# First sequence of the attention block: second half of the scores first, six banks, copies by two engines, and an order of its own up to the first ranking

## The chip, the cores and the metric

The kernel runs on one core of one Trainium2 chip. A time is the device time of one execution in microseconds (us). Before the change three runs gave a median of 3631.16 us (3630.14 to 3631.86).

## The reference

A batch of 32 sequences of 256 tokens with 128 channels passes through two blocks, all in float32. Block 0 is a state-space mixer and a feed-forward network, each followed by a layer norm. Block 1, which the change concerns, is attention and another feed-forward network:

```python
q, k, v = heads of x @ Wq, x @ Wk, x @ Wv        # 16 heads of 64
k, v = concat(mem_k, k), concat(mem_v, v)        # 4 memory columns: 260 keys
dots = einsum('bhid,bhjd->bhij', l2norm(q), l2norm(k)) * 10
dots = einsum('hg,bgij->bhij', W_pre_th, dots)   # heads are mixed
dots = where(causal, mask_value, dots)
vk = top_k(dots, 64)[..., -1:]                   # the 64th largest of a row
dots = where(dots < vk, mask_value, dots)
attn = einsum('hg,bgij->bhij', W_post_th, softmax(dots))
out = (attn @ v) * head_scale_params             # then a sigmoid gate, @ Wo
x = layernorm(x + out)
```

## The kernel before

Five engines run five programs that meet only at semaphores. `mixer_phase` (L608) does block 0 for all sequences. `attention_phase` (L1109) then does block 1, one sequence after another in a software pipeline.

Within `attention_phase` a sequence goes through these steps. PE makes the **scores** of 16 heads (`score`, L1407): queries 0 to 127 (half 0, called `blk` 0) against 132 keys in 6 pieces of two or three heads, queries 128 to 255 (half 1) against 260 keys in 16 pieces of one head, into the three banks `FRONT`. ACT copies a piece out of its bank into the buffer `SN`, scaled by the reciprocal norm of the queries (`s_keep`, L1618). SP sends `SN` to a scratch tensor in DRAM, `scores_by_token` (`stage`, L1329), in three pieces for half 0 and four for half 1, and brings it back with heads on the partitions, eight queries by sixteen heads (`regroup`, L1346 and L1348), into the buffer `T8[b % 2]`. A group is 8 queries, there are 32, and two groups form a pair of up to 512 columns. PE **premixes** a pair with W_pre (`premix`, L1422) into one bank, `MIX`; ACT copies it back into `T8` (`t_keep`, L1626); POOL adds the causal mask (`hide`, L1949). The next premix waits until the copy of the last has emptied the bank.

DVE **ranks** the masked scores: eight rankings per sequence (numbered here 0 to 7), each of a quad of four groups, two wide and two narrow. A ranking begins with a `TENSOR_REDUCE` (L1870) and two `TENSOR_TENSOR` (L1803, L1806) and goes on with `MAX8` and `MATCH_REPLACE8` until the 64th value is known. Then ACT takes the row's peak (`peaks`, L1587), POOL drops what is below the threshold (`drop`, L1974 to L1984), ACT takes the exponentials with their sums (`exps`, L1602), DVE the reciprocal of the sums (`share_out`, L1755), POOL scales W_post by it (`share_posts`, L1933), and PE mixes the heads back (L1434, L1438). A ranking waits for work of earlier ones:

```python
if k >= 2:
    dve.wait_ge(dropped, drops(k - 2, 3))
    dve.wait_ge(peaked, k - 1)
```

Beside this the next sequence is prepared: K projected by PE (`k_piece`, L448), squared and summed by ACT (L496), clipped by POOL (`k_clip`, L538), the reciprocal root by ACT and POOL, K scaled by ACT (`k_scale`, L511, tile `ktok`), turned by PE (`k_turn`, L457), all of it in two halves; then Q, whose norms PE sums in `q_turn` (L488), DVE clips in `q_clip` (L566, tile `q_sq`) and ACT and POOL turn into `rq`. The copies of the next scores need `rq`.

What orders this is a table. Each engine runs over periods `p` of 128 beats `t`, and at each beat asks of each step whether it is due (`whose(p, t, beat, lag)`, L1303). A beat is no time: it only says which instruction of an engine stands behind which. In period 1 DVE ranks sequence 0 while PE, ACT, POOL and SP prepare sequence 1; DVE's ranking is cut into 8 slots of 16 beats, and slot n holds ranking n.

For sequence 0 nothing runs beside it that fills the time: DVE waits until its scores have been made, sent, brought back, mixed and masked. `tails` (L1389 on PE, L1578 and L1579 on ACT) makes the last rows of V for all sequences; it stands ahead of the first premix and the first `t_keep`. At the start of the phase POOL clears `T8[0]`, `T8[1]`, `V2` and the three `AT` (L1920 to L1924). `peaks(0, 0)` stands behind ten `t_keep`s of sequence 0, and the remaining six are spread over the period.

Of the kernel before, what the change touches and what calls it, by code (L numbers as in the profile page):

```python
# [12 lines left out]
P = 128  # L13
# [25 lines left out]
S_ALL = len(S_PIECES[0]) + len(S_PIECES[1])  # L39
EXP_LN, SILU, GELU = "natural_log_exp_and_others", "silu_and_others", "gelu_and_others"  # L40
# [378 lines left out]
class Front:  # L419
# [3 lines left out]
    def __init__(self, sh, room, sems, banks):  # L423
# [14 lines left out]
        self.s_kept, self.first_squared = sems.sem("s_kept"), sems.sem("first_squared")  # L438

    def k_piece(self, pe, b, t, f):  # L440
        x = self.xb[b % NXB]
        if t == 0 and f == 0:
            pe.wait_ge(self.x_loaded[b % NXB], 16 * (b // NXB + 1))
            if b:
                pe.wait_ge(self.s_kept, S_ALL * b)
        if t:
            pe.wait_ge(self.k_scaled, 4 * b + f + 1)
# [661 lines left out]
def attention_phase(nc, sh, ctx, out):  # L1109
# [38 lines left out]
    PAIR_AT = {g: (blk * HALF + k) // 2 for blk in range(2) for k, g in enumerate(PREMIX[blk])}  # L1148
# [25 lines left out]

    x_loaded, y_out = front.x_loaded, sems.sems("y_out", 2)
# [4 lines left out]
    zeroed = sems.sem("zeroed")  # L1180
    q_kept, q_clipped, q_root = front.q_kept, front.q_clipped, front.q_root
    s_made, s_kept = sems.sem("s_made"), front.s_kept
# [56 lines left out]
    PE_MIX = (56, 68, 84, 111, 118, 120, 124, 138)  # L1239
    PE_OUT = 35  # L1240
# [71 lines left out]
    def sync(sp):  # L1312
# [8 lines left out]
        def stage(b, blk):  # L1321
# [5 lines left out]
            for n, (lo, hi, pieces) in enumerate(STAGES[blk]):  # L1327
                sp.wait_ge(s_kept, S_ALL * b + S_BEFORE[blk] + pieces)
                sp.dma_start(by_token[blk][:, lo:hi, 0:w], SN[:, lo:hi, 0:w]).then_inc(staged[blk][n], 16)  # L1329

        def regroup(b, blk):

            if b == 1 and blk == 0:
                sp.wait_ge(zeroed, 2)
# [4 lines left out]
            for k in range(HALF // 2):  # L1339
# [10 lines left out]
        for p in range(PERIODS):  # L1350
# [17 lines left out]
            if seq(r):  # L1368
                sp.wait_ge(v_kept, len(WV) * r + 2)
                if r == 0:  # L1370
                    sp.wait_ge(tail_in, 32)
                    sp.wait_ge(zeroed, 2)
# [5 lines left out]
    def tensor(pe):  # L1378
# [14 lines left out]
        def score(b, blk, piece):  # L1393

            n = S_BEFORE[blk] + piece
# [5 lines left out]
            if n >= 2:  # L1401
                pe.wait_ge(s_kept, S_ALL * b + n - 1)
            w = W_LO if blk == 0 else W_HI
            for j, even in enumerate(S_PIECES[blk][piece]):
                for half in range(2):
                    rows = slice(half * DH, (half + 1) * DH)
                    last = pe.matmul(FRONT[(n + half) % 3][:, j * w:(j + 1) * w], qT[rows, even // 2, blk * P:(blk + 1) * P],  # L1407
# [4 lines left out]
        def premix(b, blk, k):  # L1412

            pair = pair_scores(b, PREMIX[blk][2 * k])
            n = 2 * PAIRS * b + PAIRS * blk + k
            if n == 0:
                tails()
# [83 lines left out]

        for p in range(-1, PERIODS):
            for t in range(BEATS):
                for n in range(4):
                    if b := whose(p, t, PE_K[n], 0):
# [35 lines left out]
                for n in range(3):  # L1541
                    if (b := whose(p, t, PE_SCORE0[n], 0)) is not None:
                        score(b, 0, 2 * n)
# [3 lines left out]
                for n in range(8):  # L1547
                    if (b := whose(p, t, PE_SCORE1[n], 0)) is not None:
# [8 lines left out]
                for blk in range(2):  # L1557
                    for k in range(PAIRS):
                        if (b := whose(p, t, PE_PREMIX[blk][k], 0)) is not None:
                            premix(b, blk, k)  # L1560

    def scalar(act):
# [26 lines left out]
        def exps(b, i, pair):  # L1589
# [8 lines left out]
            else:  # L1598
                act.wait_ge(masked, HALF * b + PAIR_AT[QUAD[i][2 * pair]] + 1)
# [4 lines left out]
        def s_keep(b, blk, piece):  # L1604
# [7 lines left out]
            if b and n == 0:  # L1612
# [7 lines left out]

        def t_keep(b, blk, k):
            pair = pair_scores(b, PREMIX[blk][2 * k])
            if (b, blk, k) == (0, 0, 0):
                tails()
            act.wait_ge(premixed, 2 * PAIRS * b + PAIRS * blk + k + 1)
# [44 lines left out]

        for p in range(-1, PERIODS):
            for t in range(BEATS):
                for n in range(4):
                    if (b := whose(p, t, ACT_CTX[n], 2)) is not None:
                        ctx_keep(b, n)
                for n in range(4):
                    if b := whose(p, t, ACT_K[n], 0):
# [16 lines left out]
                for i in range(QUADS):  # L1694
                    if (b := whose(p, t, ACT_PEAK[i])) is not None:
# [21 lines left out]
                for n in range(3):  # L1717
                    if (b := whose(p, t, ACT_SCORE0[n], 0)) is not None:
# [9 lines left out]
                for n in range(8):  # L1728
                    if (b := whose(p, t, ACT_SCORE1[n], 0)) is not None:
# [375 lines left out]
```

## Time and profile before

| what | us |
|---|---|
| median of three runs | 3631.16 |
| the profiled execution, its own time | 3634.36 |
| its span, first to last instruction | 3633.1 |
| DVE busy, share of the span | 3437.1, 95% |
| PE busy | 3390.1, 93% |
| ACT busy | 3092.9, 85% |
| POOL busy | 1745.4, 48% |
| block 1 begins (first instruction of its ACT) | 810.96 |
| first wide step of ranking 0 of sequence 0 | 846.70 |
| mean granted clock of TensorE, share of full speed | 0.98 |

All stretches below are in us from the start of the span. A row of the timeline gives the start, the length of the group, engine, line, operation, output and input with their sizes, how many instructions, and in square brackets how long the engine had been idle before and what released it. A row of busy times gives a stretch, its length, the busy time (and number) of PE, of PE's weight loads, of DVE, ACT and POOL, the granted clock of TensorE as a share of 2.4 GHz, the busy share of the DMA engines and the GB/s they moved.

### The profile page before, as it was taken

Reading aid. Unit: us, or ns where it says so; the run is one execution under the profiler, and the core shown is the slowest. Engines: PE = TensorE matmul, PEld = TensorE weight load, DVE = VectorE, ACT = ScalarE, POOL = GpSimd, SP = SyncE. Lnnn points to the kernel's source line nnn. Section 1 sums busy time; section 2 is a strip of 40 time slices with the busy share of each in tenths; the row PEclk is TensorE's granted clock in tenths of the full one; section 3 lists DMA queues with packets and bytes.
Section 4 is the critical chain, followed back from the end, with each engine's and each line's share of the span. In section 5 each row is a group of like instructions: output and inputs, shape, how many; then the busy total and the mean of one; then the engine's idle time right before and its main releaser. Section 6 shows DMA issues by size and latency. Waiting matters only on the chain.

```text
span 3633.1 us, 78764 instructions
## 1 busy us (share of the span) xinstructions
PE 3390.1 (93%) x19287; PEld 2527.5 (70%) x19287; DVE 3437.1 (95%) x18664; ACT 3092.9 (85%) x10837; POOL 1745.4 (48%) x3670
## 2 busy tenths in 40 slices
PE   4999999986999999999999999999999999999987
PEld 2888888863666666676676666666666666666665
DVE  7999999936999999999999999999999999999993
ACT  6888888856898899989899898998998998898863
POOL 0000000014666666666666666666666666666663
PEclk9999999997999999999999999999999999999998
DMA  3000000002222222222222222222222222222210
GB/s 132 11 14 13 13 12 13 10 13 85 73 71 78 82 66 65 65 66 66 66 65 66 74 71 70 74 73 79 79 66 65 65 66 65 67 65 66 73 55 4
DMA packets 254141, 210.74 MB, mean 58 GB/s; under 512 B 78000, under 2 KB 234736, under 8 KB 252912
## 3 DMA queue, kind: packets, MB, share of 16 engines
q1 hardware_dynamic: 253680, 205.70, 18.1%
q8 instruction: 154, 2.52, 0.3%
q14 instruction: 307, 2.51, 0.2%
HBM read 93.97 MB, written 111.67 MB: 57 GB/s over the span
## 4 chain that ended last, share of the span: by engine, by line
PE 66%; ACT 17%; DVE 11%; issue 4%; POOL 2%; DMA 0%; SPq 0%; DVEq 0%; ACTq 0%; POOLq 0%
PE bank L378 10%; PE bank L221 8%; PE bank L1434 6%; PE bank L1422 5%; PE bank L1407 5%; PE bank L1465 3%; PE bank L469 3%; PE bank L195 3%; ACT SN L1618 3%; PE bank L1499 3%; DVE W L1826 3%; PE bank L1479 3%; PE bank L1438 3%; PE bank L346 3%; ACT sq L496 2%
## 5 line engine op out<-in xcount | busy, mean ns | idle before, releaser
L1826 DVE MATCH_REPLACE8 W<-last,W 128x130 f32<-128x130 f32 (+18 forms) x3456 | 871.9, 259 | 0.0
L1848 DVE MAX8 last<-W 128x8 f32<-128x130 f32 (+18 forms) x3456 | 762.9, 262 | 0.0
L1933 POOL TENSOR_SCALAR posts<-post,share 128x128 f32<-128x128 f32 x1024 | 366.7, 378 | 284.0 <-DVE share L1755 279.1
L1602 ACT ACTIVATE T<-T,peak 128x260 f32<-128x260 f32 (+15 forms) x1024 | 410.9, 409 | 3.5 <-POOL T L1984 2.4
L1618 ACT ACTIVATE SN<-bank,rq 128x260 f32<-128x260 f32 (+1 forms) x1024 | 357.9, 424 | 61.3 <-PE bank L1407 60.8
L1422 PE MATMUL bank<-T,pre 128*128 128x40 f32 (+15 forms) x1024 | 365.3, 439 | 14.4 <-ACT T L1626 10.1
L1434 PE MATMUL bank<-posts,T 128*128 128x128 f32 (+7 forms) x2048 | 311.7, 289 | 68.9 <-POOL posts L1933 60.6
L1984 POOL TENSOR_TENSOR T<-T,below 128x520 f32<-128x520 f32 (+12 forms) x416 | 360.3, 882 | 20.0 <-DVE below L1857 4.6
L1434 PEld LDWEIGHTS bank<-posts,T 128*128 128x128 f32 (+7 forms) x2048 | 249.0, 174 | 165.3 <-POOL posts L1933 88.9
L938 DVE TENSOR_TENSOR_SCAN hs<-dA,dx 128x256 f32<-128x256 f32 x512 | 349.9, 684 | 2.9 <-ACT dA L800 1.9
L1949 POOL TENSOR_TENSOR T<-T,w_mask 128x32 f32<-128x32 f32 x512 | 141.1, 278 | 412.6 <-ACT T L1626 410.2
L1407 PE MATMUL bank<-kT,qT 64*128 64x260 f32 (+1 forms) x2048 | 275.7, 373 | 43.3 <-ACT SN L1618 33.9
L538 POOL TENSOR_SCALAR k_sq<-k_sq 128x16 f32<-128x16 f32 x64 | 17.7, 276 | 564.7 <-DVE k_sq L551 514.3
L1974 POOL TENSOR_SCALAR below<-T,last 128x244 f32<-128x244 f32 (+3 forms) x256 | 269.6, 1053 | 33.6 <-DVE last L1846 10.3
L1422 PEld LDWEIGHTS bank<-T,pre 128*128 128x128 f32 x1024 | 168.7, 192 | 164.6 <-issue 84.6
L1826 DVE MATCH_VALUE_LOAD W<-last,W 128x8 f32 x3456 | 262.6, 76 | 0.0
L221 PE MATMUL bank<-f_b,w_f1h 128*128 128x256 f32 x1024 | 248.6, 386 | 5.7 <-ACT f_b L233 5.7
L1626 ACT ACTIVATE T<-bank 128x40 f32<-128x40 f32 (+15 forms) x512 | 208.2, 407 | 49.6 <-PE bank L1422 47.1
L1571 ACT ACT_TABLE_LOAD x192 | 246.3, 1283 | 4.6 <-POOLq L1100 1.1
L221 PE MATMUL bank<-f_a,w_f1h 128*128 128x256 f32 x1024 | 247.7, 385 | 0.0
L800 ACT ACTIVATE dA<-delta,neg_a 128x256 f32<-128x256 f32 x512 | 237.5, 502 | 8.8 <-DVE delta L1067 8.4
L1407 PEld LDWEIGHTS bank<-kT,qT 64*128 64x128 f32 x2048 | 146.9, 191 | 136.5 <-ACT SN L1618 76.2
(242 smaller groups left out, 9572.3 us busy)
## 6 DMA issues: line engine op xcount, KB each, us to landing
scores_by_token<-SN SPq DMA_DIRECT2D x64, 520.0 KB, 2.6
scores_by_token<-SN SPq DMA_DIRECT2D x64, 396.0 KB, 3.1
scores_by_token<-SN SPq DMA_DIRECT2D x32, 780.0 KB, 3.3
scores_by_token<-SN SPq DMA_DIRECT2D x32, 264.0 KB, 2.6
scores_by_token<-SN SPq DMA_DIRECT2D x32, 260.0 KB, 2.0
T<-scores_by_token SPq DMA_DIRECT2D x32, 244.0 KB, 3.0
T<-scores_by_token SPq DMA_DIRECT2D x32, 228.0 KB, 3.2
T<-scores_by_token SPq DMA_DIRECT2D x32, 212.0 KB, 3.8
```

What stands on the lines that cost most here:

```text
L221: last = pe.matmul(o[:, (m % 2) * SEQ:(m % 2 + 1) * SEQ], self.w[layer][:, c, m * P:(m + 1) * P], src[:, c, :], start=c == 0, stop=c == HC ...
L378: last = pe.matmul(o[:, (m % 2) * SEQ:(m % 2 + 1) * SEQ], self.w[layer][:, c, m * P:(m + 1) * P], src[:, c, :], start=c == 0, stop=c == HC ...
L938: dve.tensor_tensor_scan(hs[j % NH][:], dA[j % ND][:], dx[b % 2][:], 0.0, ALU.mult, ALU.add).then_inc(scanned, 1)
L1407: last = pe.matmul(FRONT[(n + half) % 3][:, j * w:(j + 1) * w], qT[rows, even // 2, blk * P:(blk + 1) * P], kT[rows, even // 2, 0:w], star ...
L1422: pe.matmul(MIX[:, 0:pair.shape[-1]], pre[:], pair, start=True, stop=True).then_inc(premixed, 1)
L1434: return pe.matmul(at0[0:m, j * P:(j + 1) * P], scores(b, QUAD[i][j], 0, m), posts[(n + j) % NP][:], start=True, stop=True)
L1602: act.activation(one, one, ACT.Exp, bias=peak[k % 2][:, j:j + 1], accum_out=total[k % 4][:, j:j + 1]).then_inc(e_made, 1)
L1618: last = act.activation(SN[:, h, 0:w], FRONT[n % 3][:, j * w:(j + 1) * w], ACT.Copy, scale=rq[:, c:c + 1])
L1826: dve.match_replace(both[:, s, at:to], best[n], both[:, s, at:to], LOWEST).then_inc(ranked, 1)
L1848: dve.max(best[n], both[:, s, at:to]).then_inc(ranked, 1)
L1933: pool.tensor_scalar(posts[(4 * k + j) % NP][:], post[:], share[k % 2][:, j:j + 1], 1.0, ALU.mult, ALU.mult).then_inc(posts_made, 1)
L1984: pool.tensor_tensor(x, x, out, ALU.add).then_inc(dropped, 1)
```

## The change

It concerns sequence 0 of block 1, and the steps of sequence 1 that are prepared beside its ranking.

1. **Scores.** Half 1 is made before half 0. Six banks are used in turn, where it was three. Even pieces are copied by ACT, odd ones by DVE, which did not copy scores. Half 0 goes to a buffer of its own, a part of `T8[1]`, so that its copies do not wait until `SN` has been sent.
2. **SP.** Half 1 is sent first (four pieces), then half 0 (three). The pairs then come back one by one, of half 1 and of half 0 in turn.
3. **Premix.** All 16 premixes, `t_keep`s and `hide`s of sequence 0 stand directly behind the scores on PE, ACT and POOL, pairs of half 1 and half 0 in turn. The first half of sequence 1's K is projected and squared ahead of them. On POOL the first `drop` stands behind the twelfth `hide`.
4. **Clearing.** `T8[1]` and `V2` are cleared by DVE, `T8[1]` once half 0 has been sent.
5. **Order behind it.** `tails` stands behind `peaks(0, 0)` on ACT and behind the last premix on PE. `peaks(0, 1)`, the first `share_out`, the first `drop` of ranking 1 and `q_clip` of sequence 1 have beats of their own.

The core of the diff:

```diff
+FIRST_SCORES = [(blk, piece) for blk in (1, 0) for piece in range(len(S_PIECES[blk]))]
...
+    FIRST = [(blk, k) for k in range(QUADS) for blk in (1, 0)]
+    FIRST_SN = (T8[1][:, 0:HEADS * W_LO].rearrange("p (h n) -> p h n", h=HEADS), SN)
+    FIRST_BANK = [*FRONT, *ATB, BACK[1]]
+    TAILS = 12
+    FIRST_PEAK, FIRST_SHARE, FIRST_CLIP = 24, 62, 68
...
             if seq(f):
-                stage(f, 0)
-                regroup(f, 0)
-                stage(f, 1)
-                regroup(f, 1)
+                if f:
+                    for blk in range(2):
+                        stage(f, blk)
+                        regroup(f, blk)
+                else:
+                    stage(0, 1)
+                    stage(0, 0)
+                    for blk, k in FIRST:
+                        regroup(0, blk, (k,))
...
+        for blk, piece in FIRST_SCORES[::2]:
+            score(0, blk, piece)
+        for f in range(2):
+            front.k_piece(pe, 1, 0, f)
+        for blk, k in FIRST:
+            premix(0, blk, k)
         for p in range(-1, PERIODS):
             for t in range(BEATS):
+                if (p, t) == (1, TAILS):
+                    tails()
...
+        first_keep()
+        for f in range(2):
+            front.k_square(act, 1, 0, f)
+        for blk, k in FIRST:
+            t_keep(0, blk, k)
...
+        dve.wait_ge(q_root.stepped, Root.STEPS)
+        for n, (blk, piece) in enumerate(FIRST_SCORES):
+            if n % 2:
+                dve.wait_ge(s_made, n + 1)
+                w = (W_LO, W_HI)[blk]
+                for j, h in enumerate(S_PIECES[blk][piece]):
+                    c = blk * HEADS + h
+                    last = dve.tensor_scalar(FIRST_SN[blk][:, h, 0:w], FIRST_BANK[n % 6][:, j * w:(j + 1) * w], rq[:, c:c + 1], None, ALU.mult)
+                last.then_inc(s_halved, 1)
+        dve.memset(V2[:], 0.0)
+        for sent in staged[0]:
+            dve.wait_ge(sent, 16)
+        dve.memset(T8[1][:], 0.0).then_inc(blanked, 1)
...
-        pool.memset(T8[1][:], 0.0)
-        pool.memset(V2[:], 0.0)
...
+        for blk, k in FIRST:
+            hide(0, blk, k)
+            if (blk, k) == (0, 5):
+                turn_over(0, 0)
+                drop(0, 0)
```

ACT, from the first `t_keep` of half 1 to the first `k_scale` (`T_0` is `T8[0]`, `peak` is the step `peaks`, `ktok` the scaled K, `k_t` and `rk` its root). Before:

```order
L1626 ACTIVATE T_0<-bank 128x512
L78 ACTIVATE k_t<-k_sq 128x16
L80 ACTIVATE rk<-k_t 128x16
L1626 ACTIVATE T_0<-bank 128x488
L1587 ACTIVATE peak<-top 128x4
L511 ACTIVATE ktok<-bank,rk 128x64 x16
```

After, from the sixth `t_keep` from the end:

```order
L1673 ACTIVATE T_0<-bank 128x360
L1673 ACTIVATE T_0<-bank 128x200
L1673 ACTIVATE T_0<-bank 128x328
L1673 ACTIVATE T_0<-bank 128x232
L1673 ACTIVATE T_0<-bank 128x296
L1673 ACTIVATE T_0<-bank 128x264
L79 ACTIVATE k_t<-k_sq 128x16
L81 ACTIVATE rk<-k_t 128x16
L1624 ACTIVATE peak<-top 128x4
L1615 ACTIVATE V<-bank 128x512
L1616 ACTIVATE V<-bank 128x512
L1624 ACTIVATE peak<-top 128x4
```

Here `L514 ACTIVATE ktok` follows directly. The root of K and the first peak stand behind all sixteen `t_keep`s, where they stood behind nine and ten; the two copies of `tails` stand ahead of `ktok`.

DVE, from the last instruction of block 0 to the first ranking (`SN` and `T_1`, which is `T8[1]`, take the copies). Before:

```order
L566 TENSOR_SCALAR q_sq<-bank 128x32
L1870 TENSOR_REDUCE top<-T_0 128x2
L1803 TENSOR_TENSOR W<-T_0 128x2x130
L1806 TENSOR_TENSOR W<-T_0 128x2x130
L1814 MAX top<-W 128x8 x2
```

After:

```order
L569 TENSOR_SCALAR q_sq<-bank 128x32
L1948 TENSOR_SCALAR SN<-bank,rq 128x260 x8
L1948 TENSOR_SCALAR T_1<-bank,rq 128x132 x8
L1950 MEMSET V 128x1024
L1953 MEMSET T_1 128x4480
L1924 TENSOR_REDUCE top<-T_0 128x2
L1857 TENSOR_TENSOR W<-T_0 128x2x130
```

Sixteen copies and two memsets stand ahead of ranking 0.

DVE in ranking 4, from its `TENSOR_REDUCE` to `q_clip` of sequence 1 (`neg` is a negated narrow group). Before:

```order
L1870 TENSOR_REDUCE top<-T_0 128x2
L1803 TENSOR_TENSOR W<-T_0 128x2x98
L566 TENSOR_SCALAR q_sq<-bank 128x32
L1806 TENSOR_TENSOR W<-T_0 128x2x98
L1814 MAX top<-W 128x8 x2
```

After:

```order
L1924 TENSOR_REDUCE top<-T_0 128x2
L1857 TENSOR_TENSOR W<-T_0 128x2x98
L1860 TENSOR_TENSOR W<-T_0 128x2x98
L1868 MAX top<-W 128x8 x2
L1880 MATCH_REPLACE W<-top,W 128x98 x2
L1824 MAX last<-neg 128x8
L1902 MAX last<-W 128x8 x2
L1832 MATCH_REPLACE W<-last,neg 128x76
L1832 MATCH_REPLACE W<-last,neg 128x84
L1880 MATCH_REPLACE W<-last,W 128x98
L569 TENSOR_SCALAR q_sq<-bank 128x32
```

`q_clip` stands behind eleven more instructions of ranking 4.

## Rows read from the trace of the kernel before

**Rows 1.** Busy time by stretches: the long middle, when DVE ranks sequences 1 to 31.

```profile
930.00:3490.00 2560.00, 2454.93 (x15015) 1761.09 (x15013) 2531.22 (x15994) 2308.68 (x8954) 1622.30 (x3429) 1.00 0.22 69
```

**Rows 2.** Timeline of DVE: rankings 0, 2 and 4, q_clip, first ranking of sequence 1.

```profile
846.70 0.43 DVE L1803 TENSOR_TENSOR W<-T 128x260 f32<-128x260 f32 x1 [21.00 <-POOL T L1949]
...
866.40 0.25 DVE L1870 TENSOR_REDUCE top<-T 128x2 f32<-128x104 f32 x1
...
883.94 0.32 DVE L1870 TENSOR_REDUCE top<-T 128x2 f32<-128x168 f32 x1
...
884.44 0.19 DVE L566 TENSOR_SCALAR q_sq<-bank 128x32 f32<-128x32 f32 x1
...
932.46 0.43 DVE L1803 TENSOR_TENSOR W<-T 128x260 f32<-128x260 f32 x1 [0.36 <-POOL T L1949]
```

**Rows 3.** Timelines of PE, ACT and POOL: scores, their copies, clearing.

```profile
811.07 0.94 PE L1407 MATMUL bank<-kT,qT 64*128 64x132 f32 x12 [1.97 <-POOLq L1100]
...
829.00 1.24 PE L1407 MATMUL bank<-kT,qT 64*128 64x260 f32 x4
...
827.20 0.85 ACT L1618 ACTIVATE SN<-bank,rq 128x260 f32<-128x260 f32 x2 [0.83 <-PE bank L1407]
...
811.21 3.83 POOL L1920 MEMSET T<- 128x4480 f32 x1
```

**Rows 4.** Timeline of SP's queue: sending half 0, bringing halves 0 and 1 back.

```profile
815.45 3.24 SPq L1329 DMA_DIRECT2D scores_by_token<-SN  x3
...
821.85 3.95 SPq L1348 DMA_DIRECT2D T<-scores_by_token  x8
...
841.50 3.50 SPq L1348 DMA_DIRECT2D T<-scores_by_token  x7
```

**Rows 5.** Busy time by stretches: sending half 0, half 1, and three of PE's.

```profile
818.00:819.00 1.00, 1.00 (x4) 0.34 (x5) 0.00 (x0) 0.30 (x2) 1.00 (x2) 0.50 1.13 288
829.00:830.00 1.00, 1.00 (x5) 0.50 (x4) 0.00 (x0) 0.28 (x1) 0.25 (x1) 0.50 1.01 424
826.00:842.00 16.00, 13.40 (x37) 6.71 (x38) 0.00 (x0) 6.89 (x19) 1.73 (x7) 0.50 0.42 155
843.00:850.00 7.00, 3.96 (x8) 0.89 (x6) 3.30 (x20) 6.07 (x40) 2.60 (x10) 1.00 0.93 287
...
863.00:867.00 4.00, 4.00 (x15) 3.13 (x13) 4.00 (x22) 2.62 (x11) 0.34 (x1) 0.54 0.01 2
```

**Rows 6.** Timelines of PE and ACT: tails, a premix at half clock, at full.

```profile
819.00 3.62 PE L1389 MATMUL bank<-w_wv,gate 128*128 128x512 f32 x4
...
837.59 1.03 PE L1422 MATMUL bank<-T,pre 128*128 128x200 f32 x2
...
844.57 1.12 PE L1422 MATMUL bank<-T,pre 128*128 128x512 f32 x2 [0.83 <-DMA T<-scores_by_token]
...
838.66 0.34 ACT L1626 ACTIVATE T<-bank 128x200 f32<-128x200 f32 x1
...
845.74 0.60 ACT L1626 ACTIVATE T<-bank 128x512 f32<-128x512 f32 x1
```

**Rows 7.** Timelines of ACT, POOL and PE: K and Q of sequence 1.

```profile
848.20 3.39 ACT L511 ACTIVATE ktok<-bank,rk 128x64 f32<-128x64 f32 x16
...
860.27 3.39 ACT L511 ACTIVATE ktok<-bank,rk 128x64 f32<-128x64 f32 x16 [0.75 <-POOL rk L90]
...
856.63 1.51 POOL L1984 TENSOR_TENSOR T<-T,below 128x520 f32<-128x520 f32 x1 [4.27 <-DVE below L1857]
...
876.84 0.51 PE L488 MATMUL bank<-w_stack,qn 128*128 128x16 f32 x4
```

**Rows 8.** Timeline of ACT: sequence 1's first copies and first `t_keep` of half 1.

```profile
886.64 1.64 ACT L1618 ACTIVATE SN<-bank,rq 128x132 f32<-128x132 f32 x6
...
907.95 0.85 ACT L1618 ACTIVATE SN<-bank,rq 128x260 f32<-128x260 f32 x2 [4.08 <-PE bank L1407]
...
930.22 0.67 ACT L1626 ACTIVATE T<-bank 128x512 f32<-128x512 f32 x1
```

More of the change, by code:

```diff
@@ L445, in k_piece @@
                 pe.wait_ge(self.s_kept, S_ALL * b)
+                pe.wait_ge(self.s_halved, S_ALL // 2)
         if t:
@@ L1327, in stage, with regroup @@
             for n, (lo, hi, pieces) in enumerate(STAGES[blk]):
[L1328 to L1331 removed]
+                if b:
+                    sp.wait_ge(s_kept, S_ALL * b + S_BEFORE[blk] + pieces)
+                else:
+                    kept = FIRST_SCORES.index((blk, 0)) + pieces
+                    sp.wait_ge(s_kept, kept)
+                    sp.wait_ge(s_halved, kept // 2)
+                by_head = SN if b else FIRST_SN[blk]
+                sp.dma_start(by_token[blk][:, lo:hi, 0:w], by_head[:, lo:hi, 0:w]).then_inc(staged[blk][n], 16)
+        def regroup(b, blk, pairs=range(HALF // 2)):
             if b == 1 and blk == 0:
[L1334 removed]
+                sp.wait_ge(blanked, 1)
             if b >= 2 and blk == 0:
@@ L1338, in regroup @@
                 sp.wait_ge(sent, 16 * (b + 1))
-            for k in range(HALF // 2):
+            for k in pairs:
                 g = PREMIX[blk][2 * k]
@@ L1406, in score @@
                     rows = slice(half * DH, (half + 1) * DH)
-                    last = pe.matmul(FRONT[(n + half) % 3][:, j * w:(j + 1) * w], qT[rows, even // 2, blk * P:(blk + 1) * P],
+                    last = pe.matmul((FRONT[(n + half) % 3] if b else FIRST_BANK[(n + half) % 6])[:, j * w:(j + 1) * w], qT[rows, even // 2, blk * P:(blk + 1) * P],
                                      kT[rows, even // 2, 0:w], start=True, stop=True)
@@ L1541, in tensor @@
                 for n in range(3):
-                    if (b := whose(p, t, PE_SCORE0[n], 0)) is not None:
+                    if b := whose(p, t, PE_SCORE0[n], 0):
                         score(b, 0, 2 * n)
@@ L1547, in tensor @@
                 for n in range(8):
-                    if (b := whose(p, t, PE_SCORE1[n], 0)) is not None:
+                    if b := whose(p, t, PE_SCORE1[n], 0):
                         score(b, 1, 2 * n)
@@ L1676, in scalar @@
                 for n in range(4):
-                    if b := whose(p, t, ACT_K[n], 0):
+                    if (b := whose(p, t, ACT_K[n], 0)) and (b > 1 or n >= 2):
                         front.k_square(act, b, n // 2, n % 2)
@@ L1694, in scalar @@
                 for i in range(QUADS):
-                    if (b := whose(p, t, ACT_PEAK[i])) is not None:
+                    if (b := whose(p, t, FIRST_PEAK if i == 1 and p == 1 else ACT_PEAK[i])) is not None:
                         peaks(b, i)
@@ L1717, in scalar @@
                 for n in range(3):
-                    if (b := whose(p, t, ACT_SCORE0[n], 0)) is not None:
+                    if b := whose(p, t, ACT_SCORE0[n], 0):
                         s_keep(b, 0, 2 * n)
@@ L1728, in scalar @@
                 for n in range(8):
-                    if (b := whose(p, t, ACT_SCORE1[n], 0)) is not None:
+                    if b := whose(p, t, ACT_SCORE1[n], 0):
                         s_keep(b, 1, 2 * n)
@@ L1898, in vector @@
                 for i in range(QUADS):
-                    if (b := whose(p, t, DVE_SHARE[i])) is not None:
+                    if (b := whose(p, t, FIRST_SHARE if i == 0 and p == 1 else DVE_SHARE[i])) is not None:
                         share_out(QUADS * b + i)
@@ L1904, in vector @@
                     nc_.dve_finish(dve, b, x_c[:])
-                if b := whose(p, t, DVE_Q_CLIP, 0):
+                if b := whose(p, t, FIRST_CLIP if p == 1 else DVE_Q_CLIP, 0):
                     front.q_clip(dve, b)
@@ L1999, in gpsimd @@
                 for i in range(QUADS):
-                    if (b := whose(p, t, POOL_TURN[i])) is not None:
+                    if (b := whose(p, t, POOL_TURN[i])) is not None and (b, i) != (0, 0):
                         turn_over(b, i)
-                    if (b := whose(p, t, POOL_DROP[i])) is not None:
+                    if (b := whose(p, t, POOL_DROP[0 if i == 1 and p == 1 else i])) is not None and (b, i) != (0, 0):
                         drop(b, i)
```

61 lines of the change are left out of this document (39 added, 22 removed).

## The prediction

> **What bounds the kernel now.** I read the busy times of the long middle first. Between 930 and 3490 DVE is busy 2531.22 of 2560 us, 98.9%, and PE 95.9% [rows 1]. So from sequence 1's first ranking to the end DVE's rankings set the pace, and the time of the kernel is the start of that ranking plus a stretch that the change does not touch. Call the first wide step of sequence 1's ranking R1: it began at 932.46 [rows 2]. **A microsecond is won only if R1 comes earlier by one.** A measurement of this kernel can tell about 0.2% from no change, which is 7.3 us.
>
> Then the timeline of DVE ahead of R1. Ranking 0 of sequence 0, call its first wide step R0, began at 846.70 after 21.00 us of idleness [rows 2]; from there to R1 DVE hardly waits. That idle time is what the change is after. The timelines of SP, PE and ACT show what it consists of: clearing before the first send, half 0 sent and brought back before half 1 is sent [rows 4], scores and copies that pass three banks, at TensorE's lower clock level [rows 3, 5]. The last thing to read is what else stands between R0 and R1: the chain that prepares K and Q of sequence 1 on the other engines [rows 7, 8]. R1 needs both.
>
> **Part 1: R0 comes about 12.7 us earlier.** The scores begin at 811.07 as before. A score group for two 260-wide pieces takes 1.24 at half clock, its two copies on ACT 0.85 [rows 3]. With six banks and two copying engines PE no longer waits for banks: 8 groups by 1.24 are 9.9 us for half 1, at full clock about half. That two engines copy means that copies follow PE. DVE's copy from a bank is in no row of before; bounds are 0 and ACT's 0.43 apiece, and neither end binds, since 8 of them by 0.43 lie beside 5 to 10 us of PE. By the errata section of the Trainium skill's page "VectorE: DVE Perf Modes" (VectorE, source in PSUM) such a copy would take (120 + 260) cycles at 0.96 GHz, 0.40 us, an estimate that leaves the sum as it is.
>
> The transfers are what is left. The queue's first send waits for POOL's first clearing, 811.21 + 3.83 = 815.04 [rows 3]; the first send was issued at 815.45 [rows 4]. Half 1 is 256 x 16 x 260 x 4 / 2 = 2.13 MB, and the part sent at 829 moved at 424 GB/s; half 0 is 1.08 MB and moved at 288 [rows 5]. From 816.1: 0.45 (another load ahead of it) + 5.0 + 3.75 = 825.3; landing and its signal add about 1, so half 0 is complete near 826.2 (with 288 GB/s for both halves 828.6, with 424 for both 825). Then the first narrow pair is issued with about 0.5 and the first wide pair, which came back 3.07 us after its issue at 841.50 (issue in [rows 4], premix at 844.57 in [rows 6]): first premix 829.8. Two pairs must be mixed before ranking 0. At half clock two matmuls of w columns take 0.36 + 0.0032w (0.0032 from the four 512-wide ones, 3.62 us; 0.36 from the 200-wide pair, 1.03), the copy 0.17 + 0.00083w (0.34 and 0.60), 0.1 for the two handovers [rows 6]. 512 columns: 2.7. 40 columns: 0.8. A mask and its handovers 0.6. **R0 = 833.9, 12.8 earlier.** DVE's clearing of `T8[1]` lies in this stretch (826.2 to at most 831.6; POOL's takes 3.83 [rows 3]) and is hidden by the transfer and the first premix; without that cover it would be 4 to 5 us.
>
> **Part 2: sequence 1's K comes later.** Before, the first peak and the root of K stood behind ten and nine `t_keep`s; now both stand behind all sixteen, and these go through one bank one after another: no premix begins before the copy of the last. Widths sum to 8 x 552 + 56 = 4472. At half clock PE takes 16 x 0.36 + 4472 x 0.0032 = 20.1, ACT 16 x 0.17 + 4472 x 0.00083 = 6.4, handovers 1.6: **28.1 us**, 829.8 to 857.9. At full clock the 512-wide pair takes 1.12 [rows 6]; with 0.30 + 0.0016w PE takes 12.0 and the chain 20.0.
>
> Which clock? In the score stretch, 13.40 us busy of 16, it stayed at 0.50; under an uninterrupted PE (863 to 867) it rose; at 843 to 850 PE was busy 57% and it stayed at 1.00 [rows 5]. The chain comes out of several idle us of PE, so it begins at the lower level, and it keeps PE at 20.1 / 28.1 = 72%, less than in the stretch that stayed low. I take half clock and keep the other as a rival.
>
> Behind the last `t_keep`: root of K and first peak by 858.9; `tails`, 3.62 on PE [rows 6] plus copies, until 861.8; then the first `ktok`, which began at 848.20 [rows 7]: **+13.6**. The second began at 860.27, 12.07 later, of which POOL's first `drop` at 856.63 held the clipping up by about 2.7 [rows 7]; that drop now lies earlier, so the second `ktok` is at 861.8 + 9.4 = 871.2, +10.9. Behind it the chain to `q_turn` (876.84) is PE's and ACT's own work; one premix of 0.8 us has left it: q_turn near 887, and q_clip can run at about 888.
>
> **Part 3: DVE waits in the middle instead.** Unhindered, DVE would reach ranking 2 at 833.9 + 19.7 = 853.6. It needs the first peak, 858.9: a wait of 5.3. Ranking 4 (883.94 - 866.40 = 17.5 later: 876.4) needs the third peak, which stands behind the turned K on ACT, near 881: 4.6. q_clip stands 2.3 us further into ranking 4 than before (eleven instructions) and would be reached at 884; it waits for q_turn until about 888: 4. Together 14 us of new waits against 12.8 won. q_clip to R1 was 932.46 - 884.44 = 48.0 with a wait of 0.36 in it; less 2.3 that now lies ahead, 45.4. **By DVE's own work R1 = 933.5, +1.**
>
> **Part 4: sequence 1's scores.** Their copies need `rq`, behind q_clip and behind the gates, which follow q_turn: they began at 886.64 [rows 8] and now begin near 895.7, +9.1. From there to the first wide `t_keep`, 930.22 [rows 8], lie 43.6 us of copies, sending and mixing. Part of that were waits for PE and POOL whose work follows DVE's rankings (these come only 1 to 3 us later), so the chain can catch up, to some +4 at the `t_keep`: R1 = 932.46 + 4 = 936.5. This is later than 933.5, so it decides. **Sum: 3631.2 + 4 = 3635.2 us**; the profiled execution, 3634.36 by its own time, would be 3638.4. I forecast 3635.
>
> **Rivals.**
> - *Full clock in the mixing chain.* The chain would end 8.1 earlier, at 849.8, first peak 850.8, ahead of ranking 2, K and Q some +3 instead of +11. R1 near 930.3: -2.2, 3629. For it: at 843 to 850 a PE busy for only 57% kept the upper level [rows 5]. Against it: the idle PE ahead of the chain. Beside this stands the Trainium skill, "TensorE: Matmul & The Clock Gate", section "HAM oscillation": matmuls in bursts with waits between them lose the upper clock and run at half of it; the row at 826 to 842 agrees for scores, the one at 843 to 850 does not.
> - *The gain holds.* If the first peak, the third peak and q_turn come before DVE asks for them, R1 moves by all of R0's 12.8: 3618.4; with half of the waits 3624. It needs the K chain to be 10 us faster than its rows; for it speaks only that the chain has gaps of 1 to 5 us in the trace which could close, and that its work is spread over more engines.
> - *Slower.* The copies of sequence 1's scores begin 9.1 late and do not catch up: their place is ACT's queue behind the gates, where each later copy has scores, exponentials and peaks of earlier rankings ahead of it. Then R1 = 932.46 + 9.1 and the time 3640.3. It decides from a catching up of less than 2 us (3638.4 is the bound of slower). For it: PE and ACT are busy 96% and 90% of the long middle [rows 1] and have little to catch up with. Against it: within those 43.6 us ACT waited 4.08 for PE at 907.95 [rows 8], and there PE was waiting in turn for work that follows DVE.
> - *It doesn't do what it says.* If sending the two halves takes turns with other traffic and R0 is only 5 us earlier, the chain of part 2 begins later too, and the time goes the slower way; it is in that case's chance.
>
> **Chances.** Forecast (half clock, R1 +1 to +7) 0.52; full clock, 3629, 0.17; gain holds wholly or by half 0.13; slower 0.18. So faster by over 0.2% 0.13, within 0.2% 0.69, slower by over 0.2% 0.18. The range takes in the first two, the half of the gain's nearer end and the price of the slower rival: 3625 to 3641.
>
> **What would show it.** R0 near 834 in DVE's timeline; sixteen premixes between 830 and 858 at a granted clock of 0.50; the first peak at 859 and DVE idle about 5 us ahead of ranking 2, again ahead of ranking 4, and before q_clip; `ktok` at 862 and 871; sequence 1's first copies near 896; R1 near 936. Wrong would be: an upper clock in the chain, DVE without waits between R0 and R1, or R1 before 928.

## The result and the profile after

Twelve runs of the change had a median of 3640.76 us, twelve of the kernel before beside them 3630.65. The ratio is **1.0024, 95% interval 1.0014 to 1.0034**, so the change costs 5 to 12 us, 8.7 at its middle. A second comparison, on another set of runs, gave 1.0025 (1.0013 to 1.0037). The median lies in the stated range (3625 to 3641) by 0.24 us. Its ratio is on the slower rival's side of the 0.2% bound, not the forecast's, though the interval reaches across that bound.

The single profiled executions hide this: 3634.36 us before, 3634.72 after. What the change does must be read ahead of R1, the first wide step of sequence 1's ranking. I give times from **start**, the first table load of the attention block on ACT (810.96 before, 810.43 after), because it moves from one execution to the next: over all thirteen profiles of this record it lies between 809.05 and 813.25.

| from start, us | before | forecast | after |
|---|---|---|---|
| R0, first wide step of ranking 0 | 35.7 | 22.9 | 23.9 |
| copy of the sixteenth pair ends | – | 46.9 | 49.0 |
| first peak | 37.0 | 47.9 | 50.3 |
| first scaled K | 37.2 | 50.8 | 53.1 |
| second scaled K | 49.3 | 60.2 | 63.5 |
| `q_clip` of sequence 1 | 73.5 | 77 | 78.8 |
| first copies of sequence 1's scores | 75.7 | 84.7 | 86.2 |
| first wide `t_keep` of sequence 1 | 119.3 | 123.3 | 126.8 |
| R1 | 121.5 | 125.5 | 129.0 |

The forecast's clock times stand here less 810.96. R1 is 7.5 us later in place of 4, and that is nearly all of the 8.7. (A second profile of each kernel, below, has 122.3 and 128.6, so R1 itself is known to some 0.8 us; the two means are 6.9 apart.)

The timeline of DVE in the kernel after, the rows with a wait and R0 (they answer to [rows 2]):

```profile
834.22 0.20 DVE L1924 TENSOR_REDUCE top<-T 128x2 f32<-128x40 f32 x1 [2.62 <-POOL T L2014]
834.33 0.42 DVE L1857 TENSOR_TENSOR W<-T 128x260 f32<-128x260 f32 x1
...
861.05 0.26 DVE L1924 TENSOR_REDUCE top<-T 128x2 f32<-128x104 f32 x1 [7.99 <-issue]
...
883.26 0.18 DVE L1809 RECIPROCAL share<-total 128x4 f32<-128x4 f32 x1 [4.62 <-ACT T L1639]
...
886.11 0.33 DVE L1924 TENSOR_REDUCE top<-T 128x2 f32<-128x168 f32 x1 [1.77 <-POOL T L2049]
...
889.24 0.19 DVE L569 TENSOR_SCALAR q_sq<-bank 128x32 f32<-128x32 f32 x1 [0.22 <-PE bank L491]
...
901.13 0.57 DVE L1911 TENSOR_SCALAR below<-T,last 128x196 f32<-128x196 f32 x2 [5.32 <-POOL T L2049]
...
939.46 0.43 DVE L1857 TENSOR_TENSOR W<-T 128x260 f32<-128x260 f32 x1 [0.34 <-POOL T L2014]
```

Read from above: R0 is 11.8 us earlier from start, as wanted. Then DVE waits 7.99 ahead of ranking 2, 4.62 for the first share, 1.77 ahead of ranking 4, 0.22 at `q_clip` and 5.32 inside ranking 4: 19.9 us at places where it had not waited in the kernel before. The profile puts the 7.99 down to no engine; the first peak on ACT ended at 860.96, just ahead of it (next view). 19.9 - 11.8 is 8.1; R1 moved by 7.5.

PE and ACT, timelines, at both ends of the row of sixteen and behind it ([rows 6, 7]):

```profile
817.88 1.96 PE L451 MATMUL bank<-w_wk,xb 128*128 128x512 f32 x4 [1.26 <-DVE T L1948]
830.14 2.07 PE L1451 MATMUL bank<-T,pre 128*128 128x512 f32 x2 [10.31 <-DMA T<-scores_by_token]
833.00 0.62 PE L1451 MATMUL bank<-T,pre 128*128 128x40 f32 x2 [0.78 <-ACT T L1673]
833.91 1.99 PE L1451 MATMUL bank<-T,pre 128*128 128x488 f32 x2 [0.29 <-ACT T L1673]
...
857.80 1.25 PE L1451 MATMUL bank<-T,pre 128*128 128x264 f32 x2 [0.51 <-ACT T L1673]
858.84 3.62 PE L1417 MATMUL bank<-w_wv,gate 128*128 128x512 f32 x4
```

```profile
859.09 0.39 ACT L1673 ACTIVATE T<-bank 128x264 f32<-128x264 f32 x1 [1.34 <-PE bank L1451]
...
860.77 0.19 ACT L1624 ACTIVATE peak<-top 128x4 f32<-128x4 f32 x1
862.50 0.60 ACT L1615 ACTIVATE V<-bank 128x512 f32<-128x512 f32 x1 [1.54 <-PE bank L1417]
...
863.57 3.38 ACT L514 ACTIVATE ktok<-bank,rk 128x64 f32<-128x64 f32 x16
...
873.88 3.38 ACT L514 ACTIVATE ktok<-bank,rk 128x64 f32<-128x64 f32 x16 [0.75 <-POOL rk L91]
```

Each premix waits for the copy of the one before, each copy for its premix. The busy times show the clock in it: PE is busy 18.95 us of 27, at 0.50 throughout:

```profile
832.00:859.00 27.00, 18.95 (x32) 7.99 (x32) 18.74 (x100) 6.06 (x15) 5.12 (x16) 0.50 0.17 45
```

Last, POOL's timeline ahead of the wait that I had not forecast, at 901.13:

```profile
895.22 0.24 POOL L85 TENSOR_TENSOR q_t<-rq 128x32 f32<-128x32 f32 x1 [9.15 <-ACT rq L81]
...
896.53 2.09 POOL L2039 TENSOR_SCALAR below<-T,last 128x212 f32<-128x212 f32 x2
898.67 0.15 POOL L2044 MEMSET below<- 128x68 f32 x1
898.92 0.52 POOL L2041 TENSOR_SCALAR below<-neg,last 128x68 f32<-128x68 f32 x1
899.52 1.51 POOL L2049 TENSOR_TENSOR T<-T,below 128x424 f32<-128x424 f32 x2
```

POOL stood idle for 9.15 us, waiting for the root of sequence 1's query norms, which comes from ACT behind the gates and two table loads. Behind that root in POOL's queue is the drop of ranking 3, whose values had been there since DVE ended that ranking at 884.3, and for that drop DVE waited.

The chain of sequence 1 on ACT, its first score copies and its first wide `t_keep` ([rows 8]):

```profile
896.63 1.64 ACT L1655 ACTIVATE SN<-bank,rq 128x132 f32<-128x132 f32 x6
...
937.24 0.68 ACT L1673 ACTIVATE T<-bank 128x512 f32<-128x512 f32 x1
```

Between them lie 40.6 us, where the kernel before had 43.6.

### The profile page after: what moved, and what is told of

It reads as the page before. It is cut to its first block, busy times and chain, and to the rows that moved or that the text cites. A ratio compares the mean times of both kernels' runs of the same rounds, so it can differ in the third digit from the quotient of the medians.

```text
span 3633.4 us, 78806 instructions
## 1 busy us (share of the span) xinstructions
PE 3381.3 (93%) x19287; PEld 2520.0 (69%) x19287; DVE 3449.5 (95%) x18682; ACT 3085.4 (85%) x10821; POOL 1732.8 (48%) x3668
## 4 chain that ended last, share of the span: by engine, by line
PE 60%; DVE 17%; ACT 16%; issue 5%; POOL 2%; DMA 0%; SPq 0%; DVEq 0%; ACTq 0%; POOLq 0%
PE bank L379 9%; PE bank L222 7%; PE bank L1463 5%; PE bank L1451 5%; DVE W L1880 5%; PE bank L1438 4%; DVE last L1902 3%; PE bank L472 3%; PE bank L1494 3%; PE bank L196 3%; PE bank L1528 3%; ACT sq L499 2%; PE bank L1508 2%; ACT SN L1655 2%; PE bank L1467 2%
## 5 line engine op out<-in xcount | busy, mean ns | idle before, releaser
L1451 PE MATMUL bank<-T,pre 128*128 128x392 f32 (+15 forms) x1024 | 371.0, 445 | 25.1 <-ACT T L1673 12.3
L1655 ACT ACTIVATE SN<-bank,rq 128x132 f32<-128x132 f32 (+1 forms) x992 | 345.6, 423 | 52.6 <-PE bank L1438 52.2
L1438 PE MATMUL bank<-kT,qT 64*128 64x260 f32 (+1 forms) x2048 | 267.7, 366 | 38.6 <-ACT SN L1655 32.3
L1673 ACT ACTIVATE T<-bank 128x512 f32<-128x512 f32 (+15 forms) x512 | 207.6, 405 | 75.8 <-PE bank L1451 73.9
L379 PE MATMUL bank<-f_b,w_f0h 128*128 128x256 f32 x1024 | 241.4, 379 | 0.0
```

What stands on the lines that cost most here:

```text
L379: last = pe.matmul(o[:, (m % 2) * SEQ:(m % 2 + 1) * SEQ], self.w[layer][:, c, m * P:(m + 1) * P], src[:, c, :], start=c == 0, stop=c == HC ...
L1438: last = pe.matmul((FRONT[(n + half) % 3] if b else FIRST_BANK[(n + half) % 6])[:, j * w:(j + 1) * w], qT[rows, even // 2, blk * P:(blk + ...
L1451: pe.matmul(MIX[:, 0:pair.shape[-1]], pre[:], pair, start=True, stop=True).then_inc(premixed, 1)
L1655: last = act.activation(SN[:, h, 0:w], FRONT[n % 3][:, j * w:(j + 1) * w], ACT.Copy, scale=rq[:, c:c + 1])
```

## The experiments

Three questions: what moves R1, which part of the front wins the 11.8 us, and why the clock stayed low. Edits are shortened, and against the change where nothing else is said. Ratios are to the kernel before; R1 and R0 are from start, from each kernel's profile (the change: 129.0 and 23.9).

### DVE's waits one by one

```diff
-if (b := whose(p, t, POOL_DROP[0 if i == 1 and p == 1 else i])) is not None ...:
+if (b := whose(p, t, POOL_DROP[0 if i == 1 and p == 1 else i] - 3 * (i == 3 and p == 1))) is not None ...:
     drop(b, i)
```

> On POOL, the drop of sequence 0's ranking 3 stands ahead of the root of sequence 1's query norms instead of behind it; nothing else differs from the change. In the profile of the change DVE waited 5.3 us for that drop inside ranking 4, at 901.13, and the drop stood in POOL's queue behind the root (895.22). Start means the first table load of the attention block on ACT (810.43 there), R1 the first wide step of sequence 1's first ranking (939.46, start + 129.0); before the change it was start + 121.5. Theory A (the scores of sequence 1 set R1, DVE's waits only fill the time until then): the 5.3 us vanish but the same time is waited at R1, R1 stays at start + 129 to 130, time about 3640. Theory B (DVE's own waits set R1): R1 at start + 123.7, time 5 us shorter, about 3635.

Ratio 1.0033 (1.0021 to 1.0045), R1 at 127.6. The 5.32 us are gone from DVE's timeline, and two others have come, 2.06 ahead of ranking 5 and 2.14 for a share just ahead of R1:

```profile
898.21 0.36 DVE L1924 TENSOR_REDUCE top<-T 128x2 f32<-128x200 f32 x1 [2.06 <-issue]
...
935.62 0.18 DVE L1809 RECIPROCAL share<-total 128x4 f32<-128x4 f32 x1 [2.14 <-ACT T L1639]
...
938.33 0.43 DVE L1857 TENSOR_TENSOR W<-T 128x260 f32<-128x260 f32 x1 [0.64 <-POOL T L2014]
```

Of 5.3 us 1.4 reach R1 (1.0 against the second profile of the change), and the time is no shorter. Removing a wait of DVE's does not move the chain of sequence 1: its first wide `t_keep` is at 126.6 from start, as in the change (126.8), and R1 can't come before it. The 1.4 lie mostly behind that `t_keep`. In the change its mask stood in POOL's queue behind a scaling of W_post that waited for DVE (937.33 to 938.75) and began at 939.18, 128.8 from start; here it begins at 127.3.

```diff
 for blk, k in FIRST:
     t_keep(0, blk, k)
+    if (blk, k) == (0, 1):
+        peaks(0, 0)
+    if (blk, k) == (0, 5):
+        peaks(0, 1)
```

> On ACT, the first two peaks of sequence 0 stand inside the row of sixteen copies (behind the fourth and the twelfth) instead of behind all of them; nothing else differs. The 8.0 us that DVE waited ahead of ranking 2 should vanish under any theory. Theory A (the chain that starts with sequence 1's K, behind the sixteen copies, sets everything until R1): the waits for the first share and ahead of ranking 4 grow by the same 8 us, R1 stays at start + 129, time about 3640. Theory B (waits of DVE add up): 8 us shorter, about 3632.

(Both peaks are taken out of the place where they stood.) Ratio 1.0035 (1.0023 to 1.0047), R1 at 130.1. Ahead of ranking 2 DVE now waits 0.71, but 3.96 in ranking 2 and 8.45 in place of 4.62 for the first share. Theory A again: R1 stays (it is 1.1 later), and the time stays with it. DVE gets no further than the chain of sequence 1 lets it.

### The row of sixteen

```diff
-pe.matmul(MIX[:, 0:pair.shape[-1]], pre[:], pair, ...)
+pe.matmul((MIX if b or n % 2 == 0 else BACK[0])[:, 0:pair.shape[-1]], pre[:], pair, ...)
```

The copy reads the same bank, and a premix waits for the copy of the pair before the last.

> The sixteen premixes of sequence 0 use two banks in turn, so that PE mixes a pair while ACT copies the one before; nothing else differs. In the change they took from 830.14 to 859.5, 29.3 us, with PE busy about 72% at half clock. Theory A (this row of sixteen, one bank, moves sequence 1's K and with it R1): at half clock the row is PE's own 20 to 21 us, the last copy near 851, sequence 1's first scaled K 8.5 us earlier, R1 7 to 8.5 us earlier (start + 121 to 122), time 3632 to 3633. If PE, now without gaps, is granted the full clock during it, the row takes about 15 and the gain is up to 12 us. Theory B (R1 is late for another reason, POOL's queue or the first rankings): R1 within 2 us of start + 129, time 3638 to 3640.

Ratio 0.9995 (0.9986 to 1.0005), **R1 at 114.0**, 15.0 us earlier than in the change by an edit that touches nothing but the row:

```profile
924.73 0.43 DVE L1857 TENSOR_TENSOR W<-T 128x260 f32<-128x260 f32 x1 [0.36 <-POOL T L2014]
```

The row takes 16.3 us in place of 29.3, and the first scaled K is at 38.9 in place of 53.1. With smaller gaps PE also got its upper clock:

```profile
834.00:838.00 4.00, 3.58 (x8) 1.85 (x6) 4.00 (x25) 0.82 (x3) 0.46 (x2) 0.50 0.71 194
838.00:842.00 4.00, 3.23 (x10) 1.70 (x8) 3.96 (x22) 1.57 (x5) 1.21 (x4) 0.78 0.01 2
842.00:846.00 4.00, 3.29 (x12) 2.10 (x13) 3.96 (x20) 1.95 (x7) 2.75 (x7) 1.00 0.02 6
```

So the expectation's case with the upper clock is the one that came, and its "up to 12 us" was too low. How the 15 us divide between overlap and clock was not measured apart; at half clock the expectation had 7 to 8.5.

Undoing that part, only ten pairs in a row and six where they stood before:

```diff
-for blk, k in FIRST:
+for blk, k in FIRST[:10]:
     t_keep(0, blk, k)
...
+    elif b == 0 and blk and k >= 2:
+        t_keep(0, *FIRST[8 + k])
```

(the same on PE and POOL, where the first `drop` stands behind the tenth `hide`)

> Undoes one part of the change: only the first ten of sequence 0's sixteen premixes, copies and masks stand in a row, the last six stand at the beats at which the last six stood before the change (one bank, as in the change). Start is the first table load of the attention block, R1 the first wide step of sequence 1's first ranking: start + 121.5 before the change, + 129.0 in the change. Theory A (sequence 1's K waits behind the row, and everything until R1 follows it): the row ends 11 us earlier, near start + 38, the first scaled K begins near + 42.5 instead of + 53.1, R1 at + 119 to 121, 8 to 10 us less than in the change, time a little below the kernel before (3622 to 3630 where that gives 3626 to 3631). Theory B (the total of the sixteen counts, wherever they stand, because the later six delay K's second half and Q by as much): R1 at + 126 or later, time 5 us or more above the kernel before.

R1 at 121.8, 7.2 earlier than in the change; first scaled K at 44.5. Theory A in kind, but 1 to 3 us less than it had said. The ratio, 1.0016 (1.0008 to 1.0025), missed the expectation by more: R1 stands where it stood in the kernel before, and the runs are 3 to 9 us longer. I come back to this below.

### The clock

```diff
+for _ in range(12):
+    pe.matmul(ATB[0][:], pre[:], sh.wv[:, 0:512], start=True, stop=True)
 for blk, k in FIRST:
     premix(0, blk, k)
```

> Twelve more matmuls of 512 columns into a free bank, whose results nobody reads, stand on PE between the K projection and the first premix, where PE idled for 10.3 us; nothing else differs. They keep PE busy until about 829.5 if the clock is full all along. Theory A with the clock as its cause: the row of sixteen starts at the full clock, and at a share of busy time of about 60% keeps it; it takes 20 to 22 us instead of 29.3, R1 is 6 to 8 us earlier, time about 3633. Rival (the clock falls inside the row, because PE has a gap behind every pair): the granted clock drops to 0.50 within the first few pairs, the row takes 27 us or more, R1 and the time stay within 2 us of the change, 3638 to 3640.

Ratio 1.0026 (1.0015 to 1.0036), R1 at 128.0. The added matmuls ended 1.2 us later, from start, than the change's first premix began. The row, now 27.1 us, did begin at the full clock, and lost it:

```profile
834.00:838.00 4.00, 2.67 (x7) 0.84 (x6) 2.37 (x6) 1.02 (x3) 0.51 (x2) 1.00 0.95 261
838.00:842.00 4.00, 2.54 (x4) 0.99 (x4) 3.96 (x26) 1.15 (x3) 0.51 (x2) 0.56 0.57 152
842.00:846.00 4.00, 2.94 (x6) 1.43 (x6) 4.00 (x21) 0.78 (x2) 0.88 (x3) 0.50 0.00 0
```

The rival was right: this row, with a gap behind each pair, did not keep the clock that it was given. The Trainium skill's page "TensorE: Matmul & The Clock Gate", section "A second HAM failure mode: psum-queue depth-cycling", tells of a kernel in which PE cycles through banks with small idle times between groups of matmuls and goes back and forth between its two clock levels. The trace agrees with the fall; here there is one, from 1.00 at 834 to 838 to 0.50 at 842 to 846, and no rise after it until the row ends. My prediction's rival of a full clock in the mixing chain is thereby excluded twice, in the change itself and with a warm start.

### K out from behind the row

```diff
+front.k_guess(act, 1, 0)
+front.k_scale(act, 1, 0)
+front.k_keep(act, 1, 0, 0)
 for n, (blk, k) in enumerate(FIRST):
     t_keep(0, blk, k)
+    if n == 1:
+        front.k_square(act, 1, 1, 0)
...
+    if n == 8:
+        front.k_scale(act, 1, 1)
```

(and the matching steps on PE and POOL)

> Against the change, sequence 1's K is taken out from behind the row of sixteen premixes: its first half is rooted, scaled and turned in the ten us in which PE and ACT wait for the first pair, its second half in ACT's gaps within the row; the first peak stands behind the eighth copy. One bank, as in the change. Theory A: the wait of 8.0 us ahead of ranking 2 is gone, the first share and ranking 4 come without most of their waits, Q's norms are turned near start + 64 to 68 instead of + 78, and R1 comes at + 112 to 116, 13 to 17 us earlier than in the change and 6 to 9 earlier than before it. R0 moves by less than 1.5. Time 3620 to 3624 where the kernel before gives 3630. Rival: the row of sixteen itself, now longer through K's steps in it, delays the second peak, the masks and Q as much as before; R1 at + 122 or later and no gain against the kernel before.

Ratio 0.9991 (0.9983 to 1.0000), R1 at 115.3, R0 at 22.95. 13.7 us come back though the row still takes until start + 51: it is not the length of the row that costs but K behind it. (The first peak, too, stands inside the row here; the early peaks alone moved nothing.) R0 even came 1 us earlier.

With that, two banks in the row and the drop of ranking 3 ahead of the root on POOL:

> The one before, with the sixteen premixes in two banks in turn and with the drop of ranking 3 ahead of the root of sequence 1's query norms on POOL. DVE's own work from R0 (start + 23.2) to R1 is 85.5 us, so R1 can be at + 108.7 at the earliest. With sequence 1's K, Q and scores all early, theory A expects R1 at + 109 to 112, 10 to 12 us earlier than in the kernel before, and a time 8 to 12 us below it. If R1 stays at + 114 as with two banks alone, something other than K and the row holds sequence 1's scores back: the exponentials, gates and table loads in ACT's queue.

**Ratio 0.9977 (0.9966 to 0.9987), median 3616.79: the fastest version, 5 to 12 us below the kernel before.** R0 at 23.1, R1 at 109.3, and of the 86.2 us between them only two waits of 2.4 us in all are no work:

```profile
833.40 0.42 DVE L1876 TENSOR_TENSOR W<-T 128x260 f32<-128x260 f32 x1
...
871.54 0.33 DVE L1943 TENSOR_REDUCE top<-T 128x2 f32<-128x168 f32 x1 [1.76 <-POOL T L2068]
...
919.63 0.43 DVE L1876 TENSOR_TENSOR W<-T 128x260 f32<-128x260 f32 x1 [0.61 <-POOL T L2033]
```

The first scaled K now lies in the time in which ACT waited for the first pair, the second between two copies:

```profile
825.62 3.40 ACT L514 ACTIVATE ktok<-bank,rk 128x64 f32<-128x64 f32 x16 [1.23 <-POOL rk L91]
...
841.06 3.39 ACT L514 ACTIVATE ktok<-bank,rk 128x64 f32<-128x64 f32 x16 [0.17 <-POOL rk L91]
```

### The front

```diff
-if n % 2 == 0:
+if True:
     act.wait_ge(s_made, n + 1)
```

(DVE makes no copy)

> Against the change, ACT makes all copies of sequence 0's scores and DVE none; the six banks, the order of the halves and all else stay. Copies by ACT were 0.43 and 0.28 us apiece, sixteen of each: 11.5 us instead of 5.9 beside DVE's. If the transfers bound this stretch (they are issued from start + 4.5 on and move half 1 in 5 us, half 0 in 3.7), R0 comes 0 to 1.5 us later than in the change (start + 23.9) and the time is that of the change, 7 to 11 above the kernel before. If the copies bound it, R0 comes 4 to 6 us later, near + 29, and R1 with it later by up to that.

Ratio 1.0016 (1.0007 to 1.0025), R0 at 24.6, R1 at 129.0. The copies by DVE are worth 0.65 us of R0 at most (a second profile of the change has R0 at 24.3) and nothing of R1: with six banks the transfers bound the front, as forecast. The time came out lower than expected, 5.8 us above the kernel before in place of 7 to 11.

```diff
-FIRST_BANK = [*FRONT, *ATB, BACK[1]]
+FIRST_BANK = [*FRONT]
...
-if n >= 6 and b == 0:
-    pe.wait_ge(s_kept, n - 4)
+if n >= 2 and b == 0:
+    pe.wait_ge(s_kept, n - 1)
```

(against the variant just told)

> Against the variant in which ACT makes all copies of sequence 0's scores, the scores pass three banks instead of six, as before the change. What is left of the change at the front is the order of the halves, the buffer of its own for half 0 and the dense row of sixteen. In that variant R0 was at start + 24.55. If transfers bound the front: R0 at + 24.5 to 26. If banks bound it (PE waits for a copy after every second piece, 1.8 us per two pieces of half 1 at half clock as in the kernel before): half 1 alone takes 14 us, its last send is issued near + 15.5, half 0 follows, R0 at + 28 to 31. R1, which follows the row of sixteen, is later than in the change by what R0 is later, start + 130 to 136, and the time 8 to 15 us above the kernel before.

Ratio 1.0037 (1.0024 to 1.0051), R0 at 33.0, R1 at 138.0. Three banks bind, and harder than I had allowed: 8.4 us of R0, where I had expected 3.5 to 6.5. PE waits 0.56 behind every second piece at the lower clock, and ACT is asked once per 1.8 us:

```profile
811.12 0.71 PE L1435 MATMUL bank<-kT,qT 64*128 64x260 f32 x4 [1.97 <-POOLq L1102]
812.84 1.24 PE L1435 MATMUL bank<-kT,qT 64*128 64x260 f32 x4 [1.01 <-ACT SN L1664]
814.63 1.24 PE L1435 MATMUL bank<-kT,qT 64*128 64x260 f32 x4 [0.56 <-ACT SN L1664]
816.43 1.24 PE L1435 MATMUL bank<-kT,qT 64*128 64x260 f32 x4 [0.56 <-ACT SN L1664]
```

With six banks all 64 score matmuls took 6.08 us at the full clock (810.53 to 816.6 in the kernel after). Of the 11.8 us of R0 8.4 thus hang on the banks where ACT makes all copies; with three banks all the rest of the front wins 3 (33.0 against 35.7). Half 1 first by itself, and three banks with two copying engines, were not run.

### The same kernels again

> The kernel before, once more, for a second profile of it. Between R1 (932.46) and the end of its span lay 2700.6 us in the first profile; in the nine profiles of the change and its variants it was 2687 to 2702, and mostly 2694 to 2696. If the stretch behind R1 differs only from execution to execution, this profile has R1 at start + 121.5 within 0.3 and a stretch behind it anywhere in 2687 to 2702, and the ratio is 1.000 within 0.001. If the first profile's 2700.6 is a property of the kernel before, it comes again, and then the change would have won some 5 us behind R1.

Ratio 1.0001 (0.9991 to 1.0010), R1 at 122.3 from start, 0.8 later than in the first profile, more than the 0.3 I had allowed. The stretch from R1 to the end of the span was 2692.6 us in place of 2700.6: it changes by 8 us between executions of one kernel. That is why the two profiled executions could come out alike: the change's has 2693.9 behind an R1 that is 7.0 us later from the start of the span.

> The change itself, once more, beside the same runs of the kernel before as the variants. R1 at start + 129.0 within 0.3. By R1 alone (7.5 us later than before, the start equal) the time is 7.5 us above the kernel before, ratio 1.0015 to 1.0030 with the first comparison's 1.0024 in it. If it comes out under 1.001 or over 1.0035, the comparison moves from set to set by more than its interval says.

Ratio 1.0025 (1.0013 to 1.0037), R1 at 128.6, 0.1 outside what I had allowed. The first result repeats.

## Why the prediction was right, and where not

**What bounds.** Right. Over the ten changed kernels (the change and its nine variants) R1 went from 109 to 138 from start, and the time followed it: 8 us below the kernel before at the one end, 13 above at the other (with a scatter that the last paragraph tells).

**Part 1, R0.** Right in kind and within 1 us (12.8 forecast, 11.8 measured from start). The microsecond lies in the transfers: half 0 had landed 16.4 us from start, when SP sent for the first narrow pair, and 15.2 was the forecast. No row of before has the 1 us that the sum takes for landing, or the 0.6 for a mask and its handovers (it was 0.4 to 0.5). The half clock that I had assumed for the scores as one of two cases did not come; six banks kept it at full. The cover of DVE's clearing held.

**Part 2, K.** Right. The row took 29.3 us against 28.1, at 0.50, and the first scaled K moved by 15.9 against 13.6 and the second by 14.1 against 10.9. K behind the row is shown to be the cause of the late R1: two banks in it, or K ahead of it, return 15.0 and 13.7 us of R1, and both together with POOL's order 19.7.

**Part 3, DVE in the middle.** The sum was 14 and is 19.9. Ahead of ranking 2 it was 8.0 in place of 5.3, mostly because the first peak came 2.4 later from start. The 4.6 ahead of ranking 4 and the 4 at `q_clip` came out as 1.77 and 0.22, with a wait of 4.62 ahead of them that the sum does not have, for the first share. And it took "q_clip to R1" for work of DVE's own, 45.4 us; that holds a wait of 5.32 for POOL, where a drop that could have run stands behind a root that could not yet. I had listed the rankings' waits for peaks, not the drops' place in POOL's queue: also ranking 4 did not start at the third peak, forecast for 881, but at 886.11, when the drop behind the first share's posts was done.

**Part 4, the scores of sequence 1. This is the step that failed**: "the chain can catch up, to some +4 at the `t_keep`". The copies began 10.5 us late and, at the first wide `t_keep`, 7.5 were left: the chain caught up 3.0 us, not 5. The copies themselves began 1.4 later than the 9.1 forecast. That term has no working; `q_turn`'s own 10.2, less the 1.86 us that ACT waited for `q_clip` in the kernel before, would be 8.3.

The reason given for catching up failed with the size. It was that DVE's rankings, on which waits in this stretch hang, would come only 1 to 3 us later. Ranking 5 came 7.4 us later from start in the change. With the drop ahead of the root it came 3.7 later, and the chain was no faster for it: its first wide `t_keep` is at 126.6 in place of 126.8. In all eleven profiles of changed kernels the stretch from the first copies to that `t_keep` is 40.6 to 41.6 us, and R1 follows the first copies by 42.0 to 42.9, whether DVE waits 0.6 us in it (K ahead and two banks) or 5.7 (peaks early). The two profiles of the kernel before have 43.6 and 45.0, and 45.8 and 46.0. So catching up more was not held up by DVE. Which steps of the chain became some 3 us shorter than before is not shown.

My two limits, DVE's and the scores', came out together (+8.1 and +7.5), not 3 apart. The slower rival was nearer in the number, 3640.3, but not in its mechanism: it said no catching up from 9.1, and it was 3.0 from 10.5. So it is in part luck that the median is inside the range: the range's upper end is that rival's price. In the rival "the gain holds" the 3624 for half of the waits is also off by a microsecond; its terms, 12.8 won and 7 waited, give 3625.4.

**Left open.** Counted from the R1 of the kernel before (121.9, the mean of its two profiles), the ratios put the changed kernels on average some 3 us higher than their R1 says (from 3 lower to 6 higher; the drop ahead of the root, two banks and ten pairs are the three near 6). The profiles do not show where: behind R1 they have 2687 to 2702 us, the kernel before 2693 and 2701. With one profile a kernel and an execution's own 8 us I can't tell whether something small is lost behind R1 or whether the ratios scatter beyond their intervals.

## What to carry to other kernels

When a start-up phase is hurried, list what stands behind the hurried work in each engine's queue. Here twelve microseconds were won at the first user and lost again, because the next item's K stood behind a row of sixteen of which the first user needed only two. Idle time ahead of a first result is where the next item's chain belongs. And a row of dependent pairs through one bank cost twice here: the gaps themselves, and the upper clock, which came only without the longer of them. A second free bank brought R1 15 us forward.

## What the hardware showed that was not expected

- A share of busy time alone did not tell whether the upper clock is kept. At 843 to 850 PE was busy 57% at 1.00 [rows 5]; in the row with a warm start it was busy 67% at 834 to 838 and the clock fell to 0.50 in the four microseconds after.
- Nor whether it comes. The row through two banks rose from 0.50 to 1.00 behind four microseconds with PE busy 3.58 of 4. In the kernel before, PE was busy 3.61 of 4 with scores and premixes at 826 to 830, and the next four stayed at 0.50.
- Six banks kept the scores at the full clock, 6.08 us for all of them; with three the first group still took 0.71 us, the second, behind a wait of 1.01 for its bank, 1.24 (at 811.12 and 812.84 above).
- Executions of one kernel differ by 8 us behind R1, with DVE busy almost all the time, as much as the whole effect that was to be judged.
